# The routed feed-forward and the choice of tokens of a three-layer hybrid kernel, put into one stage

## Time and profile before

| | us |
|---|---|
| time, median of 3 runs | 5769.16 |
| lowest and highest | 5764.76 and 5770.94 |
| the profiled execution's own time | 5774.45 |
| its span | 5772.7 |
| the last two stages in it, from the first load of `t` to the end | 497.1 |

### The profile page before, as it was taken

One profiled execution on the slowest core, in us unless ns is written; L12 is line 12 of the kernel. 1 busy time (PEld: TensorE's weight loads), 2 busy tenths in 40 slices (PEclk: granted clock), 3 DMA queues, 4 the chain that ended last, 5 costly groups with the idle time before them and its releaser, 6 DMA issues. The chain is left out here.

```text
span 5772.7 us, 84105 instructions
## 1 busy us (share of the span) xinstructions
PE 5223.8 (90%) x23692; PEld 3069.8 (53%) x23692; DVE 3456.3 (60%) x4336; ACT 2394.0 (41%) x5287; POOL 3087.8 (53%) x1607
## 2 busy tenths in 40 slices
PE   8799999999999999999997896999979889887970
PEld 4456555555555555555554444565545555554540
DVE  3477776767767677776775445555434444452228
ACT  3255555555555555555554121333323333332420
POOL 0089899898999989999897011555540000000001
PEclk9799999999999999999998888999989999998985
DMA  6511111111111111111112565022220000001121
GB/s 222 182 44 44 26 38 37 44 44 37 35 30 44 44 39 31 38 38 44 39 30 70 139 181 145 24 60 61 61 70 11 22 16 22 22 11 40 49 111 51
DMA packets 244613, 330.97 MB, mean 57 GB/s; under 512 B 87260, under 2 KB 224754, under 8 KB 234490
## 3 DMA queue, kind: packets, MB, share of 16 engines
q1 hardware_dynamic: 244218, 326.08, 20.2%
HBM read 202.49 MB, written 123.51 MB: 56 GB/s over the span
## 5 line engine op out<-in xcount | busy, mean ns | idle before, releaser
L658 POOL TENSOR_TENSOR diff_run_pool<-diff_run_pool,diff_probs 128x768 f32<-128x768 f32 x1152 | 2249.9, 1953 | 113.5 <-ACT diff_probs L506 24.8
L586 DVE TENSOR_REDUCE diff_maxes<-diff_max 128x1 f32<-128x768 f32 x1752 | 1571.1, 950 | 726.4 <-PE diff_max L408 725.4
L506 ACT ACTIVATE diff_probs<-diff_ring 128x384 f32<-128x384 f32 x3462 | 1399.0, 495 | 866.2 <-PE diff_ring L398 856.1
L434 PE MATMUL diff_out_ps<-diff_probs,diff_vs 128*64 128x384 f32 x6912 | 1253.1, 498 | 0.0
L398 PE MATMUL diff_ring<-diff_qs,diff_ks 97*128 97x384 f32 x3462 | 1074.3, 384 | 17.7 <-issue 9.3
L408 PE MATMUL diff_max<-diff_ks,diff_qs 96*128 96x384 f32 x3504 | 948.2, 352 | 39.2 <-DMA diff_vs<-v_rows 31.7
L398 PEld LDWEIGHTS diff_ring<-diff_qs,diff_ks 97*128 97x128 f32 x3462 | 606.1, 188 | 546.0 <-issue 355.1
L434 PEld LDWEIGHTS diff_out_ps<-diff_probs,diff_vs 128*64 128x64 f32 x6912 | 447.9, 137 | 546.6 <-issue 343.0
L2091 POOL MEMSET pick_before<- 128x128 f32 x1 | 0.2, 204 | 1310.5 <-POOLq L63 1310.5
L408 PEld LDWEIGHTS diff_max<-diff_ks,diff_qs 96*128 96x128 f32 x3504 | 609.6, 192 | 82.2 <-issue 32.5
L1307 DVE TENSOR_REDUCE causal_maxes<-causal_max 128x1 f32<-128x384 f32 x522 | 281.0, 552 | 317.2 <-PE causal_max L1185 191.7
(11 more groups left out here) (230 smaller groups left out, 6039.5 us busy)
## 6 DMA issues: line engine op xcount, KB each, us to landing
diff_qs<-qk_hi SPq DMA_DIRECT2D x68, 288.0 KB, 4.3
diff_ks<-qk_hi SPq DMA_DIRECT2D x68, 288.0 KB, 6.0
diff_recip<-row_factors SPq DMA_DIRECT2D x194, 96.0 KB, 2.7
o_rows<-diff_normed SPq DMA_DIRECT2D x97, 192.0 KB, 1.9
qk_hi<-proj_hi SPq DMA_DIRECT2D x12, 1536.0 KB, 5.8
qk_lo<-proj_lo SPq DMA_DIRECT2D x12, 1536.0 KB, 9.6
causal_qa<-qk_hi SPq DMA_DIRECT2D x120, 96.0 KB, 2.5
diff_qs<-qk_lo SPq DMA_DIRECT2D x34, 288.0 KB, 5.3
```

The source lines that it names most:

```text
L434: mm = pe.matmul(out_ps[VD * j:VD * (j + 1), 0:T], vs[par][:, g, j, :], probs[g % PBUF][:, j * T:(j + 1) * T], start=g == 0, stop=g == STE ...
L506: act.activation(probs[g % PBUF][:, j * T:(j + 1) * T], ring[bank][:, 0:T], ACT.Exp, scale=SCALE).then_inc(s_taken, 1)
L586: dve.tensor_reduce(maxes[side][:, row:row + 1, h], max_ps[u % 2][:, :, 0:T], AX.XY, ALU.max).then_inc(s_red, 1)
L658: pool.tensor_tensor(run_pool[:], acc[:], probs[g % PBUF][:], ALU.add).then_inc(s_accp, 1)
```

## The change

The two stages become one, `routed_ffn(nc, a, t_t, logits, factors, out)`. All 12 `x` and `base` stay in SBUF, and `delta` is written over `x`; the DRAM tensors `base_t` and `delta_t` are gone.

It has two phases. In the first, 14 steps (`s`) run a pipeline over the items: mean of item s, variance of item s-1, logit of item s-2. The logit's weight is `wr` repeated to 128 columns, so the logits arrive on all partitions at once, in `row`. Five pieces of feed-forward are put between the steps (`early`): both halves of the hidden layer of item 0, its second layer, and the hidden layer of item 1. In the second phase (`late`) only the rest of the feed-forward is left on TensorE and ScalarE, with four small transposes between, while VectorE ranks both batches and then merges item by item. The loops are written out; there is no loop instruction in the stage. The output tiles of the feed-forward share a ring of 4 PSUM banks. GpSimd has no merge any more. The rank's instructions themselves are the same.

```diff
-def routed_ffn(nc, a, t_t, logits, base_t, delta_t):
+def routed_ffn(nc, a, t_t, logits, factors, out):
...
+    ITEMS = B * NC
+    LANES, RING = 4, 4
+    KEPT = N // 2 - 1
+    FIRST, WEIGHTS = 3, 5
+    early = {3: (("hidden", 0, 0),), 5: (("hidden", 0, 1),), 7: (("ffn", 0, 0),), 9: (("hidden", 1, 0),),
+             11: (("hidden", 1, 1),)}
+    late = []
+    for n in range(2, ITEMS + 1):
+        if n == 8:
+            late.append(("factor", 0, 0))
+        if n == ITEMS - 1:
+            late.append(("factor", 1, 0))
+        if n < ITEMS:
+            late.append(("hidden", n, 0))
+        if n == 2:
+            late.append(("turn", 1, 0))
+        if n < ITEMS:
+            late.append(("hidden", n, 1))
+        late.append(("ffn", n - 1, 0))
+    tile_at = {}
+    for name, n, half in [e for s in sorted(early) for e in early[s]] + late:
+        for m in range({"hidden": 4, "ffn": KC}.get(name, 0)):
+            tile_at[name, n, 4 * half + m] = len(tile_at)
...
+        br = sb("br", [P, 1])
+        t = [sb(f"t{i}", [P, KC, T]) for i in range(LANES)]
+        dev, sq = ([sb(f"{n}{i}", [P, KC, T]) for i in range(2)] for n in ("dev", "sq"))
+        x = [sb(f"x{n}", [P, KC, T]) for n in range(ITEMS)]
+        base = [sb(f"base{n}", [P, KC, T]) for n in range(ITEMS)]
+        hid = [sb(f"hid{i}", [P, FF, T]) for i in range(2)]
+        row = [sb(f"row{i}", [P, N]) for i in L]
+        mean_ps = [ps(f"mean{i}", [P, 512]) for i in range(2)]
+        var_ps = [ps(f"var{i}", [P, 512]) for i in range(2)]
+        ring = [ps(f"ring{i}", [P, 512]) for i in range(RING)]
...
+                def load(n):
+                    sp.dma_start(t[n % LANES][:], t_t[n // NC].rearrange("(k p) n -> p k n", p=P)[:, :, columns(n)]
+                                 ).then_inc(s_ld[n % LANES], 16)
+                load(0)
+                sp.dma_start(mean_mat[:], a["mean_mat"]).then_inc(s_first, 16)
+                for n in range(1, LANES):
+                    load(n)
+                sp.dma_start(wr[:], a["wr"]).then_inc(s_first, 16)
+                sp.dma_start(br[:], a["br"][0].partition_broadcast(P)).then_inc(s_first, 16)
+                for dst, src in ((w1, a["w1"]), (b1, a["b1"]), (w2, a["w2"]), (b2, a["b2"]), (ident_sb, a["ident"])):
+                    sp.dma_start(dst[:], src).then_inc(s_w, 16)
+                for n in range(LANES, ITEMS):
+                    sp.wait_ge(s_base, n - LANES + 1)
+                    load(n)
                 for i in L:
+                    sp.wait_ge(s_row, (i + 1) * NC)
+                    sp.dma_start(logits[i:i + 1, :], row[i][0:1, :]).then_inc(s_kept[i], 16)
+                    sp.wait_ge(s_kept[i], 16)
+                    sp.dma_start(by_tile[i][:], logits[i].rearrange("(t p) -> t p", p=P)).then_inc(s_bt[i], 16)
                 for i in L:
+                    sp.wait_ge(s_frow, i + 1)
+                    sp.dma_start(factors[i].rearrange("(t p) -> t p", p=P), factor_row[i][:]).then_inc(s_fkept[i], 16)
+                    sp.wait_ge(s_fkept[i], 16)
+                    sp.dma_start(row[i][:], factors[i].partition_broadcast(P)).then_inc(s_spread[i], 16)
+                for n in range(ITEMS):
+                    sp.wait_ge(s_done, n + 1)
+                    sp.dma_start(out[n // NC].rearrange("(k p) n -> p k n", p=P)[:, :, columns(n)], base[n][:]
+                                 ).then_inc(s_out, 16)
+                sp.wait_ge(s_out, ITEMS * 16)
...
+                def mean(n):
+                    pe.wait_ge(s_ld[n % LANES], (n // LANES + 1) * 16)
+                    if n >= 2:
+                        pe.wait_ge(s_dev, n - 1)
+                    for k in range(KC):
+                        mm = pe.matmul(mean_ps[n % 2][:, 0:T], mean_mat[:], t[n % LANES][:, k, :],
+                                       start=k == 0, stop=k == KC - 1)
+                    mm.then_inc(s_mean, 1)
+                def var(n):
+                    pe.wait_ge(s_sq, n + 1)
+                    if n >= 2:
+                        pe.wait_ge(s_row, n - 1)
+                    for k in range(KC):
+                        mm = pe.matmul(var_ps[n % 2][:, 0:T], mean_mat[:], sq[n % 2][:, k, :],
+                                       start=k == 0, stop=k == KC - 1)
+                    mm.then_inc(s_var, 1)
+                def logit(n):
+                    pe.wait_ge(s_x, n + 1)
+                    for k in range(KC):
+                        mm = pe.matmul(var_ps[n % 2][:, 0:T], wr[:, k:k + 1].broadcast_to([P, P]), x[n][:, k, :],
+                                       start=k == 0, stop=k == KC - 1)
+                    mm.then_inc(s_logit, 1)
+                def feed_forward(name, n, half):
+                    if name == "turn":
+                        pe.wait_ge(s_w, 16 * WEIGHTS)
+                        pe.wait_ge(s_bt[n], 16)
+                        pe.wait_ge(s_dev, ITEMS)
+                        pe.transpose(mean_ps[n][:, 0:NT], by_tile[n][:], ident_sb[0:NT, 0:NT]).then_inc(s_turned, 1)
+                    elif name == "factor":
+                        pe.wait_ge(s_factor, n + 1)
+                        pe.transpose(mean_ps[n][0:NT, 128:128 + P], factor[n][:], ident_sb[:]).then_inc(s_back, 1)
+                    else:
+                        hidden = name == "hidden"
+                        src, w = (x[n], w1) if hidden else (hid[n % 2], w2)
+                        deep = KC if hidden else FF
+                        if hidden:
+                            pe.wait_ge(s_x, n + 1)
+                            pe.wait_ge(s_w, 16 * WEIGHTS)
+                        else:
+                            pe.wait_ge(s_taken, tile_at["hidden", n, FF - 1] + 1)
+                        for m in range(4 if hidden else KC):
+                            at_m = 4 * half + m
+                            at = tile_at[name, n, at_m]
+                            if at >= RING:
+                                pe.wait_ge(s_taken, at - RING + 1)
+                            for k in range(deep):
+                                mm = pe.matmul(ring[at % RING][:, 0:T], w[:, k, at_m * P:(at_m + 1) * P], src[:, k, :],
+                                               start=k == 0, stop=k == deep - 1)
+                            mm.then_inc(s_tile, 1)
+                for s in range(ITEMS + 2):
+                    if s < ITEMS:
+                        mean(s)
+                    if 1 <= s <= ITEMS:
+                        var(s - 1)
+                    if s >= 2:
+                        logit(s - 2)
+                    for work in early.get(s, ()):
+                        feed_forward(*work)
+                feed_forward("turn", 0, 0)
+                for work in late:
+                    feed_forward(*work)
...
+                def square(n):
+                    act.wait_ge(s_dev, n + 1)
+                    if n >= 2:
+                        act.wait_ge(s_var, n - 1)
+                    act.activation(sq[n % 2][:], dev[n % 2][:], ACT.Square).then_inc(s_sq, 1)
+                def root(n):
+                    act.wait_ge(s_var, n + 1)
+                    if n >= 2:
+                        act.wait_ge(s_rstd, n - 1)
+                    act.activation(std[n % 2][:], var_ps[n % 2][:, 0:T], ACT.Sqrt, bias=eps[:, 0:1]).then_inc(s_std, 1)
+                def keep_logit(n):
+                    act.wait_ge(s_logit, n + 1)
+                    act.activation(row[n // NC][:, columns(n)], var_ps[n % 2][:, 0:T], ACT.Identity, bias=br[:, 0:1]
+                                   ).then_inc(s_row, 1)
+                def feed_forward(name, n, half):
+                    if name == "turn":
+                        act.wait_ge(s_turned, n + 1)
+                        act.activation(col[n][:], mean_ps[n][:, 0:NT], ACT.Copy).then_inc(s_col, 1)
+                    elif name == "factor":
+                        act.wait_ge(s_back, n + 1)
+                        act.activation(factor_row[n][:], mean_ps[n][0:NT, 128:128 + P], ACT.Copy).then_inc(s_frow, 1)
+                    elif name == "hidden":
+                        act.wait_ge(s_w, 16 * WEIGHTS)
+                        if n >= 2 and half == 0:
+                            act.wait_ge(s_tile, tile_at["ffn", n - 2, KC - 1] + 1)
                         for m in range(4):
+                            at_m = 4 * half + m
+                            at = tile_at[name, n, at_m]
+                            act.wait_ge(s_tile, at + 1)
+                            act.activation(hid[n % 2][:, at_m, :], ring[at % RING][:, 0:T], ACT.Gelu_apprx_tanh,
+                                           bias=b1[:, at_m:at_m + 1]).then_inc(s_taken, 1)
+                    else:
+                        act.wait_ge(s_base, n + 1)
                         for m in range(KC):
+                            at = tile_at[name, n, m]
+                            act.wait_ge(s_tile, at + 1)
```

(70 more changed lines are left out.)

258 lines of the change are left out of this document (32 added, 226 removed).

## The result

| us | before | after |
|---|---|---|
| median of the runs (4 each) | 5770.05 | 5615.55 |
| lowest to highest | 5764.76 to 5777.49 | 5608.70 to 5617.68 |
| the profiled execution's own time | 5774.45 | 5616.61 |
| its span | 5772.7 | 5614.9 |
| the stage or stages touched, first issue to the end | 497.1 | 336.5 |

The ratio is 0.9729, with a 95% interval of 0.9712 to 0.9746. The forecast was 5609, in a range of 5597 to 5645; 154.5 us were gained (median to median) where 160.7 had been worked out.

What follows compares the result with a forecast made beforehand. Two stages with opposite bounds, TensorE then VectorE, stood one behind the other. Gaining 173.4 us at the end and giving back 12.7 nets 160.7; from 5774.45 that is 5613.8, less 5.3 for the median: 5609 us, range 5597 to 5645.

Steps and rivals of the forecast that it cites:

- behind the last matmul: End of the stage: last bias, multiplications, addition and store take 8.7 us in place of 182.1, a gain of 173.4.
- first matmul after the first issue: Start of the stage: two more loads of `t` ahead of the first weights, 1.2 us later, bounds 1.1 and 4.
- first phase, first matmul to last logit: The step pipeline, with opening, table loads and second-layer step, takes 100.4 us, bounds 97 and 108.
- plain step: First phase: chain through VectorE and ScalarE of 6.98 us, with six hand-overs of 0.04, 7.2 us.
- step with the second layer in it: First phase, step 7: 32 instructions hold up the next mean, so 12.1 us instead of 7.2.
- late turn of batch 1: Second phase: the second turn waits for the last logit's store and reload, 0 to 4 us, taken as 1.
- clock at the start of the second phase: TensorE, mostly idle for 10 us before, opens the second phase slowly: 1.8 us, bounds 0 and 4.
- 21 blocks of the second phase, transposes: Second phase on TensorE: 672 instructions of 0.323 us, 217.1 us, plus four transposes, 1 us.
- The cover of the ranks: Second phase: both rankings, 64 us each, run on VectorE under the feed-forward with some 60 us to spare.
- the low clock in the first phase: Rival, 12%: short gaps at every step lower TensorE's clock; 5664 us if always low, 5624 if half.
- slower than before: Rival, 2%: TensorE stays at 1.2 GHz in the second phase too; 5904 us if all 912 instructions do.
- the ranks don't run beside the feed-forward: Rival, 2%: the column or a semaphore comes late, so 128 us come back, 5737 us.

Runs made afterwards that it cites:

- rank1_twice: The changed kernel with VectorE counting the ranks of batch 1 twice, same result: 5615.30 us, 0.9721 of the kernel before; stage 344.6 us.
- weights_first: The changed kernel with `wr` and `br` issued ahead of the loads of items 1 to 3: 5604.65 us, 0.9705 of the kernel before; stage 332.6 us.
- split_ffn: The changed kernel with item 0's second layer halved, six early 16-instruction pieces at every second step: 5606.26 us, 0.9706 of the kernel before.
- ranks_after: The changed kernel with VectorE's ranks started only after the feed-forward's last matmul: 5758.04 us, 0.9975 of the kernel before; stage 485.5 us.
- no_early: The changed kernel with all five early feed-forward pieces moved to the head of the second phase: 5630.21 us, 0.9751 of the kernel before.

## Why the prediction was right

The stage was worked out to become 160.7 us shorter and became 160.6 shorter. The mechanism was right; that the number came out so closely is luck, since two errors of almost 4 us cancelled. By its own steps:

| step | predicted | measured |
|---|---|---|
| behind the last matmul | 182.1 to 8.7 | 182.1 to 9.0 |
| first matmul after the first issue | 1.2 later | 4.9 later (5.2 to 10.1) |
| first phase, first matmul to last logit (measured: to the first transpose) | 100.4 | 99.6 |
| plain step | 7.2 | 6.92 |
| step with the second layer in it | 12.1 | 12.35 |
| late turn of batch 1 | 1 | no wait |
| clock at the start of the second phase | 1.8 | 1.5, in the last logit, so in the 99.6 above |
| 21 blocks of the second phase, transposes | 218.1 | 217.8 |
| first to last matmul | 321.3 | 317.4 |

- **The cover of the ranks** was right: 64 us each, no wait at the transposes, 59.5 and 57.6 us to spare where some 60 had been read off, and `rank1_twice` found the bottom of it. With the reason: in the changed kernel all 72 short comparisons of the rankings take 352 ns in the mean, with TensorE and ScalarE running beside them.
- **The mis-sized term** is the start, "1.2 later, bounds 1.1 and 4". It cost 4.9, outside the bounds. The issue came 1.15 later, as said; but the landing of `br` took 6.8 us in place of 3.1. `weights_first` gives back 3.0 of these 3.7 by the order alone. The bound of 4 leaves 2.8 beside the 1.2 for the bytes of the two added loads, which is what one transfer of 384 KB by itself takes to land; it was too low. The other 0.7 is within what the landings of `br` scatter by from run to run.
- **A plain step** was 0.3 shorter, because two of its six hand-overs are from an instruction to the next on the same engine and are less than nothing: the subtraction starts 0.87 us after the start of the `base` addition ahead of it, which takes 0.96, and the root 0.75 after the square, which takes 0.84. The four others are 0.03 to 0.04, as taken. 10 steps make 3 us. A step behind a hidden half had 1.4 more instead of 1.28, and 0.2 to 0.3 of mean held up.
- **The turn of batch 1** did not wait: the logits' store took 1.4 us (5388.83 to the next issue at 5390.22) and the columns were there when TensorE came, at 5393.7.
- **The clock** fell once in the phase, where it was expected. The last logit was late by a gap of 3.64 us and took 2.93 us at 1.2 GHz for its four instructions, instead of 1.45. Behind it almost nothing was lost: from the first turn to the second it is 5.57 us here and 5.52 in `split_ffn`, where the clock is full. Between the opening and that wait TensorE's clock was full.
- These errors cancelled by chance: 3.7 lost at the start, 3.9 won between the first and the last matmul.
- **The 6.5 us between forecast and median** are not in the stage as profiled. In the profiled pair, 2.8 us of them stand ahead of the stage (5275.6 to 5278.4), in unchanged code. Then the forecast put the median 5.3 under the profiled execution, as it is before, and after the change it is 1.1 under it. Both are of the size by which the starts of the stage scatter; what makes these vary was not tried.

Of the rivals, the low clock in the first phase and its extreme, slower than before, did not happen in the changed kernel (1.00 from 5295 to 5385, and from 5390 on); the low stretch behind the first logit, in four of the other runs, is far from the 15 to 55 us that the rival was priced at. That the ranks don't run beside the feed-forward is what `ranks_after` built on purpose. The prediction priced it at 5737, as 128 us; it cost 142 in the medians and 149 in the stage, since the merges of 12 items stand bare too, 23 us, which the sum for that rival had forgotten.

## What to carry to other kernels

Where two stages with different bounds stand one behind the other, look for what of the second needs only a thin slice of the first; here the ranks need the logits alone, and putting all logits first made 128 us of VectorE's work free. Count the cover in the queue of the engine that waits for the result, not in busy shares. When a pipeline bound by a chain through several engines runs ahead of a dense phase of TensorE, nearly every idle microsecond of TensorE in it is paid: fill it with dense work, a small piece in every step (here 5.2 us in steps that had 3 us idle), even where the steps get longer by it.

## What the runs showed of the hardware that was not expected

- A 0.5 KB broadcast behind 1.2 MB of loads on the same queue landed in 6.8 us (6.0 to 7.1 in six executions), and in 3.8 and 5.0 ahead of them; a 9 KB store behind two stores of 1152 KB held up its successor for 4.0 us instead of 1.25.
- TensorE kept 2.4 GHz for 67 us at 60% busy with gaps of 1.0 to 1.6 us and one of 2.27, but waits of 2.10 to 2.23 us ahead of the first logit, of 3.64 us at the end of the first phase and of 4.66 us before a transpose each left instructions behind them at 1.2 GHz; the last two cost 1.5 and 2.2 us. A wait of 2.27 us (`no_early`) kept the clock and one of 2.10 (`split_ffn`) did not, so the length of the wait alone does not decide.
- Comparisons of 128 columns on VectorE that read two tensors took 2.2 to 5.1 us beside GpSimd's multiplications and additions and 0.35 without; beside a full TensorE and ScalarE they took 0.35. Comparisons that read one tensor kept their length beside GpSimd.
